# A two-layer transformer on one core: loops written out, first DMAs in a new order, and tile 1's first attention and layer 1's folding moved into tile 0's U and G steps

## The chip, the core and the metric

The kernel runs on one core of a Trainium2 chip. The metric is the device time of one execution in microseconds, which is the median of several runs. A profile is one further execution, with a trace of every engine: TensorE (PE, its weight loads PEld), VectorE (DVE), ScalarE (ACT), GpSimd (POOL) and SyncE (SP), which here issues all DMAs.

## The reference

The input is x, 16 tiles of 512 tokens x 256 values, float32. With `ln` the layer norm without weights:

```
x = x + A0(ln x)    A0: q,k,v = x Wq^T+bq, x Wk^T, x Wv^T+bv; 16 heads of 16; phi(t) = silu(t * 16^-0.25) + 1
                        kv = sum over tokens of phi(k) v; out = phi(q) kv; out Wo^T + bo
x = x + F0(ln x)    F0: h = silu((x w1^T) s1) * ((x w2^T) s2)        256 -> 1024, w ternary
                        h = gelu((h h1^T) s3); h = gelu((h h2^T) s4)  1024 -> 1024 -> 1024
                        (h w3^T) s5                                   1024 -> 256
x = x + A1(ln x)    A1: one head over the tile's 512 tokens: softmax(q k^T / 16) v, then w_out
x = x + F1(ln x)    F1: tanh(x W a1 a2 + bias)
```

## The kernel before

The 16 tiles are independent. A tile's work is cut into steps, and each engine walks the same list of steps, in order, doing its own share of each. The letters before a colon say for which tile a step is: `a` and `n` the next tile's first attention and the start of its F0, none the present tile's F0, `c` the tile before, whose layer 1 is computed. Since each engine runs its queue in order, a step's place in the list sets what stands in front of what.

F0 takes a tile in two halves of 256 tokens. U steps (4 for a half) multiply by w1 and w2, G steps by h1, H steps by h2, W by w3. A float32 factor is split into a high and a low float32r part (ACT, DVE and POOL do so), and PE multiplies both: 16 matmuls of 256 columns in a U step, 16 x 2 in a G, H or W step. BST, BNO and BT are statistics, normalising and transposing of a half; AST, ANO, T, AKV0 to 3, AS, AQ, AM, AO the first attention; CST to CF layer 1. PSUM has two rings of four banks, `ffn_fill` (F0) and `att_fill` (all else); a semaphore of each bank tells when it is full and when it was taken (lines 346 to 367).

PROLOGUE computes tile 0's first attention, splits the weights of it (PREP) and folds layer 1's weight matrices into each other (FOLD0, WIDE, TAKE0, FOLD1, TAKE1: products of W, a1, a2, of w_q with w_k, of w_v with w_out). FIRST is tile 0's F0 with tile 1's first attention. Then a loop of 14 passes (`nc.Fori`, line 333) walks BODY, whose semaphore values and tile slots are computed in registers from the pass's number; then LAST and TAIL come, straight, with constants. PE has the whole of that twice, in an `If` (line 1036) and its `Else`: once with float32 matmuls and once with float32r matmuls.

Which one is taken is decided by the data. The five big weights go from their input to a scratch tensor in HBM (`bounce`) and from there to SBUF (`land`). LOOK steps then read the low halves of 2048 elements of each partition: DVE takes the maximum of 1280 (line 708), ACT the sum of squares of 768 (line 789). CHECK0 to CHECK3 (w1 and w2, h1, h2, w3) add these up over the partitions with one matmul by ones, DVE writes a flag (line 712), and PE loads it into a register (`value_load`, line 829) before the first step that uses the layer, and branches on it in each step of FIRST (line 830). These weights are ternary, so the float32r form runs.

SP issues all DMAs in order. They share one queue. It waits for a `bounce` before the `land` of the same weights. x is in four slots of SBUF, and the raw weights of layer 1 are in the slots of tiles 1 to 3 until FOLD is through; hence x of tiles 1 to 3 is loaded after that. The core's lines: 510 to 523 layer norm, 563 and 728 the split after T, 575, 580 and 737 U on DVE and ACT, 584, 586 and 746 G and H, 493 POOL's low part in U, 602, 603 and 751 AKV, 635 AO, 671 CF, 688 to 703 TAKE; on PE 808 all products of `product`, 847 G and H, 863 and 871 transposes, 905 W.

The list of a pass, PLAN, which is BODY; FIRST is its steps without those of `c`, each with its looks behind it:

```python
    U0 c:CST U1 U2 U3 c:CNO G0 c:T c:CB c:CQ G1 c:CV c:CZ G2 c:CS0 G3 c:CP0 c:CS1 c:CS2 c:CO0 c:CP1 c:CS3
    H0 c:CO1 c:CP2 H1 c:CO2 BST1 c:CP3 BNO1 a:AST H2 c:CO3 c:DST H3 BT1 c:DNO W0 c:T a:ANO U0 U1 c:CF a:T
    U2 U3 a:AB a:AKV0 a:AKV1 a:AKV2 G0 a:AKV3 G1 G2 a:AS a:AQ a:AM G3 a:AO H0 H1 n:BST0 n:BNO0 H2 H3 n:BT0
    W1
```

Of the kernel before, what the change touches and what calls it, by code (L numbers as in the profile page):

```python
# [34 lines left out]
P = 128  # L35
D = 256
# [102 lines left out]
def with_checks(steps, behind):

    out, behind = [], dict(behind)
    for s in steps:
        out.append(s)
        out += steps_from(behind.pop(s[:2], ""))
    return out
# [48 lines left out]
def before(value):  # L194
# [4 lines left out]
PROLOGUE = steps_from("""  # L199
    a:AST a:ANO a:AB PREP a:T a:AKV0 SCALE a:AKV1 a:AKV2 a:AKV3 a:AS a:AQ a:AM a:AO FOLD0 WIDE  # L200
    n:BST0 n:BNO0 TAKE0 n:BT0 FOLD1 LOOK00 TAKE1 LOOK01 CHECK0 LOOK10 LOOK11""")
FIRST = with_checks(only("", "a", "n"), {
    ("U", 1): "LOOK12", ("U", 2): "LOOK13", ("U", 3): "CHECK1", ("G", 0): "LOOK20", ("G", 1): "LOOK21 LOOK22",
    ("G", 2): "LOOK23", ("G", 3): "CHECK2 LOOK30", ("H", 0): "CHECK3"})
BODY = PLAN
# [4 lines left out]
def build(nc, a):  # L210
    with ExitStack() as ctx:
# [3 lines left out]
        def sem(name):  # L215
            return ctx.enter_context(nc.semaphore(name))
# [51 lines left out]

        values = [sb("values_hi", [P, NB, D], F32R), m_parts[:].rearrange("p h k d -> p (h k) d")]
        prob = kv_b[:].rearrange("p (r a) d -> p r (a d)", r=2)  # L270
        prob_t = hi_lo("prob_t", [P, NB, P])
        kv = sb("kv", [P, KD, P])
# [14 lines left out]
        raw_wq = gated[:, 0]  # L287
        raw = [x[:, 1 + n // 2, 2 * (n % 2):2 * (n % 2) + 2, :] for n in range(6)]
        raw_q, raw_k, raw_v, raw_out, raw_f, raw_a1 = raw
        spare = whole[:].rearrange("p a b n -> p (a b n)")  # L290
        raw_a2 = spare[:, 0:512].rearrange("p (k n) -> p k n", k=KD)
        t1 = gated[:, 1]
        bk_wide = spare[:, 512:768].rearrange("p (k n) -> p k n", k=KD)
        bv_wide = spare[:, 768:1024].rearrange("p (k n) -> p k n", k=KD)
        squares = kv_b[:].rearrange("p a d -> p (a d)")

# [3 lines left out]
        s = {n: sem(n) for n in names}  # L300
        x_loaded, x_stored = sem("x_loaded"), sem("x_stored")
        a_loaded, c_loaded, small_loaded = sem("a_loaded"), sem("c_loaded"), sem("small_loaded")
        w_bounced = [sem(f"{n}_bounced") for n in CHECKED]
        w_loaded = [sem(f"{n}_loaded") for n in CHECKED]
        consts, wide, all_checked = sem("consts"), sem("wide"), sem("all_checked")
# [25 lines left out]

        def walk_rest(eng, part):
            with nc.Fori(0, T - 2, engines=[eng.engine], hint_back_edge=True) as it:
                steps_of(part, BODY, Counts(phases[2], rate, it),
                         {"c": eng.snap(it % SLOTS), "": eng.snap((it + 1) % SLOTS),
                          "a": eng.snap((it + 2) % SLOTS), "n": eng.snap((it + 2) % SLOTS)})
            steps_of(part, LAST, Counts(phases[3]), {"c": (T - 2) % SLOTS, "": (T - 1) % SLOTS})
            steps_of(part, TAIL, Counts(phases[4]), {"c": (T - 1) % SLOTS})

        def walk(eng, part):  # L340
            walk_first(part)
            walk_rest(eng, part)

# [50 lines left out]
        @block.sync  # L394
        def _(sp):
            sp.dma_start(x[:, 0], x_in[0]).then_inc(x_loaded, 16)
            sp.dma_start(raw_wkv[:, :, 0:D], km("wk0T")).then_inc(a_loaded, 16)
            sp.dma_start(raw_wkv[:, :, D:2 * D], km("wv0T")).then_inc(a_loaded, 16)
            sp.dma_start(raw_wq, km("wq0T")).then_inc(a_loaded, 16)
            sp.dma_start(wo[:], km("wo0T")).then_inc(a_loaded, 16)  # L400
            sp.dma_start(rows[:, 0:5, :], a["rows"][None].broadcast_to([P, 5, D])).then_inc(small_loaded, 16)
            sp.dma_start(cols[:], a["cols"]).then_inc(small_loaded, 16)
            sp.dma_start(scales[:], a["scales"]).then_inc(small_loaded, 16)


            parts = [[("w1T", w12[:, 0]), ("w2T", w12[:, 1])], [("h1T", h1[:])], [("h2T", h2[:])], [("w3T", w3[:])]]

            def bounce(layer):
                for name, _ in parts[layer]:
                    sp.dma_start(a["scratch_" + name], a[name]).then_inc(w_bounced[layer], 16)  # L410

            def land(layer):
                sp.wait_ge(w_bounced[layer], 16 * len(parts[layer]))
                for name, tile in parts[layer]:
                    sp.dma_start(tile.bitcast(F32), a["scratch_" + name].rearrange("(k p) n -> p k n", p=P))\
                      .then_inc(w_loaded[layer], 16)

            for tile, name in ((raw_q, "L1_attn_w_q"), (raw_k, "L1_attn_w_k"), (raw_v, "L1_attn_w_v"),
                               (raw_out, "woutT"), (raw_f, "wfT"), (raw_a1, "L1_ffn_aux_weight1"),
                               (raw_a2, "L1_ffn_aux_weight2")):  # L420
                sp.dma_start(tile, km(name)).then_inc(c_loaded, 16)
            bounce(0)
            bounce(1)
            land(0)
            land(1)
            bounce(2)
            land(2)
            bounce(3)
            land(3)

            c = Counts(phases[0])
            for step in PROLOGUE:
                if step[:2] == ("FOLD", 1):
                    wait_taken(sp, c, "att_fill", 2)
                c.ahead(step)
            for t in range(1, SLOTS):
                sp.dma_start(x[:, t], x_in[t]).then_inc(x_loaded, 16)
                sp.wait_ge(x_loaded, 16 * (t + 1))

            with nc.Fori(0, T - SLOTS, engines=[sp.engine], hint_back_edge=True) as t:  # L440
                slot = sp.snap(t % SLOTS)
# [12 lines left out]
        def _(pool):  # L454
# [623 lines left out]
```

## Time and profile before

| | us |
|---|---|
| runs | 2123.40, 2119.36, 2122.65 (median 2122.65) |
| the profiled execution's own time | 2121.59 |
| its span in the profile | 2119.2 |

| engine | PE | PEld | DVE | ACT | POOL |
|---|---|---|---|---|---|
| busy, us | 2012.3 | 1935.5 | 1208.2 | 837.6 | 372.9 |

The span runs from the first to the last instruction of the profile; the own time has 2.4 us more. The mean granted clock of PE is 0.986 of the full one. Times in the views are microseconds from the start of the span. A row of windows gives the length, then busy time and instructions of PE, PEld, DVE, ACT, POOL, the granted clock, the DMA share and GB/s. "idle before <-releaser" is the time for which an engine had nothing running and what ended it; "issue" stands for time in which it waited for nothing that the profile shows. "PEldq" is PE's sequencer, which hands the instructions to the array.

### The profile page before, as it was taken

The page shows a single profiled execution, that of the slowest core. Times are in us where ns is not written, and L with a number is a line of the kernel's source. Part 1 is how long each engine was busy: PE and PEld are TensorE (multiplying, and loading weights), DVE is VectorE, ACT ScalarE, POOL GpSimd, SP SyncE. Part 2 cuts the span into 40 slices and gives each one's busy share as a digit, 9 for nine tenths or more (in the row PEclk, how much of TensorE's full clock was granted, in tenths as well). Part 3 has the DMA queues.
Part 4 walks back from the last instruction along what each step waited for, and adds up shares of the span by engine and source line. Part 5 has one row for each costly group of instructions (what it writes and reads, how often), then busy time and mean ns, then how long its engine had stood idle before and what let it go on. Part 6 is the DMA issues. An engine that isn't in the chain of part 4 may idle for free.

```text
span 2119.2 us, 40188 instructions
## 1 busy us (share of the span) xinstructions
PE 2012.3 (95%) x15484; PEld 1935.5 (91%) x15484; DVE 1208.2 (57%) x2881; ACT 837.6 (40%) x1538; POOL 372.9 (18%) x347
## 2 busy tenths in 40 slices
PE   6899999999999999999999999999999999999985
PEld 5898999999999998999999999998999999999985
DVE  5555656465565645656366564655656466565544
ACT  2334434344443434434344343444434344343422
POOL 1111211012121021211012121121211112121011
PEclk9999999999999999999999999999999999999997
DMA  9400000000000000000000000000000000000000
GB/s 365 180 3 2 21 1 11 11 1 21 1 21 2 1 21 2 21 1 11 11 1 21 2 21 1 1 21 1 21 1 1 21 1 11 2 11 1 2 11 10
DMA packets 24402, 45.99 MB, mean 22 GB/s; under 512 B 1152, under 2 KB 21376, under 8 KB 24064
## 3 DMA queue, kind: packets, MB, share of 16 engines
q1 hardware_dynamic: 24240, 43.41, 5.8%
q8 instruction: 153, 2.51, 0.5%
q14 instruction: 9, 0.07, 0.0%
HBM read 35.02 MB, written 19.92 MB: 26 GB/s over the span
## 4 chain that ended last, share of the span: by engine, by line
PE 80%; DVE 7%; POOL 4%; issue 4%; DMA 3%; ACT 2%; SPq 0%; DVEq 0%; POOLq 0%; ACTq 0%
PE ffn_fill L847 43%; PE att_fill L808 23%; PE ffn_fill L905 6%; PE ffn_fill L808 5%; POOL act_lo L493 3%; DVE whole L575 2%; PE att_fill L863 2%; PE att_fill L981 1%; DMA scratch_h2T<-in_h2T 1%; DMA scratch_h1T<-in_h1T 1%; POOL rstd_C L480 1%; DVE st L510 1%; DVE act_hi L580 1%; DMA h<-scratch_h2T 1%; PE ffn_fill L871 1%
## 5 line engine op out<-in xcount | busy, mean ns | idle before, releaser
L847 PE MATMUL ffn_fill<-act_hi,h 128*128 128x256 f32 x4096 | 989.5, 284 | 9.6 <-POOL act_lo L493 4.1
L847 PE MATMUL ffn_fill<-act_lo,h 128*128 128x256 f32 x4096 | 980.4, 281 | 0.0
L847 PEld LDWEIGHTS ffn_fill<-act_hi,h 128*128 128x128 f32 x4096 | 773.3, 189 | 17.0 <-POOL act_lo L493 7.3
L847 PEld LDWEIGHTS ffn_fill<-act_lo,h 128*128 128x128 f32 x4096 | 774.7, 189 | 3.7
L584 DVE CAST act_hi<-whole 128x512 fp32r<-128x512 f32 x256 | 109.9, 429 | 570.8 <-ACT whole L746 570.8
L746 ACT ACTIVATE whole<-ffn_fill,scales 128x256 f32<-128x256 f32 x512 | 215.2, 472 | 553.7 <-PE ffn_fill L847 552.8
L808 PE MATMUL ffn_fill<-half_hi,w 128*128 128x256 f32 x1024 | 260.7, 294 | 39.7 <-issue 29.9
L808 PE MATMUL ffn_fill<-half_lo,w 128*128 128x256 f32 x1024 | 255.3, 288 | 0.0
L808 PEld LDWEIGHTS ffn_fill<-half_hi,w 128*128 128x128 f32 x1024 | 201.2, 196 | 45.0 <-issue 35.2
L493 POOL TENSOR_TENSOR act_lo<-whole,act_hi 128x512 fp32r<-128x512 f32 x128 | 166.9, 1304 | 405.3 <-DVE act_hi L580 404.7
L480 POOL TENSOR_TENSOR rstd_B<-var_eps_B,minus_half 128x2 f32<-128x2 f32 x32 | 22.7, 709 | 1131.5 <-DVE var_eps_B L517 1131.5
L808 PEld LDWEIGHTS ffn_fill<-half_lo,w 128*128 128x128 f32 x1024 | 201.3, 197 | 0.0
L586 DVE TENSOR_TENSOR act_lo<-whole,act_hi 128x512 fp32r<-128x512 f32 x256 | 190.9, 746 | 8.8
L746 ACT ACT_TABLE_LOAD x92 | 118.0, 1283 | 163.2 <-PE ffn_fill L847 143.4
L737 ACT ACTIVATE gated<-ffn_fill,scales 128x256 f32<-128x256 f32 x256 | 105.9, 473 | 159.7 <-PE ffn_fill L808 159.0
L575 DVE SCALAR_TENSOR_TENSOR whole<-ffn_fill,scales,gated 128x256 f32<-128x256 f32 x256 | 111.8, 478 | 69.9 <-PE ffn_fill L808 64.6
L905 PE MATMUL ffn_fill<-w,act_hi 128*128 128x256 f32 x512 | 123.8, 285 | 0.0
L905 PE MATMUL ffn_fill<-w,act_lo 128*128 128x256 f32 x512 | 121.1, 279 | 0.0
L905 PEld LDWEIGHTS ffn_fill<-w,act_lo 128*128 128x128 f32 x512 | 96.6, 189 | 0.0
L905 PEld LDWEIGHTS ffn_fill<-w,act_hi 128*128 128x128 f32 x512 | 96.1, 188 | 0.0
L510 DVE BATCH_NORM_STATS2 st<-x 128x6 f32 (+1 forms) x256 | 91.2, 414 | 6.6 <-DMA x<-in_L_attn_x 5.0
L475 POOL TENSOR_TENSOR x<-x,rows 128x512 f32 (+1 forms) x64 | 85.2, 1352 | 21.0 <-DVE xn L523 18.0
(156 smaller groups left out, 3156.0 us busy)
## 6 DMA issues: line engine op xcount, KB each, us to landing
x<-in_L_attn_x SPq DMA_DIRECT2D x16, 512.0 KB, 3.8
out<-x SPq DMA_DIRECT2D x16, 512.0 KB, 3.7
h<-scratch_h1T SPq DMA_DIRECT2D x1, 4096.0 KB, 16.2
h<-scratch_h2T SPq DMA_DIRECT2D x1, 4096.0 KB, 13.8
w<-scratch_w1T SPq DMA_DIRECT2D x1, 1024.0 KB, 14.4
w<-scratch_w2T SPq DMA_DIRECT2D x1, 1024.0 KB, 16.5
w<-scratch_w3T SPq DMA_DIRECT2D x1, 1024.0 KB, 5.6
rows<-in_rows SPq DMA_DIRECT2D x1, 640.0 KB, 5.9
```

The source lines that it names most:

```text
L475: last = pool.tensor_tensor(xs[:, b:b + 2, :], xs[:, b:b + 2, :], row2(bias_row), ALU.add)
L480: pool.tensor_tensor(rstd_of[stage][:, :nb], var_eps_of[stage][:, :nb], minus_half[:, :nb], ALU.pow)\
L493: pool.tensor_tensor(act_lo[0][:, blocks], whole[:, n % WHOLES], act_hi[0][:, blocks].bitcast(F32), ALU.subtract).then_inc(s["ffn_ready"], 1)
L510: last = dve.bn_stats(st[:, b, :], xs[:, b, :])
L575: last = dve.scalar_tensor_tensor(whole[:, n % WHOLES, o, :], two(bank)[:, o, :], scales[:, 1, 2 * j + o:2 * j + o + 1], gated[:, j % 2, o ...
L584: dve.tensor_copy(act_hi[dst][:, blocks], whole[:, n % WHOLES]).then_inc(s["hi_ready"], 1)
L586: dve.tensor_tensor(act_lo[dst][:, blocks], whole[:, n % WHOLES], act_hi[dst][:, blocks].bitcast(F32), ALU.subtract).then_inc(s["ffn_ready ...
L737: last = act.activation(gated[:, j % 2, o, :], two(bank)[:, o, :], ACT.Silu, scale=scales[:, 0, 2 * j + o:2 * j + o + 1])
L746: last = act.activation(whole[:, n % WHOLES, o, :], two(bank)[:, o, :], ACT.Gelu, scale=scales[:, layer, 2 * j + o:2 * j + o + 1])
L808: last = pe.matmul(out, lhsT, rhs, start=n == 0, stop=n == len(pairs) - 1)
L847: last = pe.matmul(two(bank)[:, o, :], view(w), view(moving[:, k, :]), start=k == 0 and o == 0 and half == 0, stop=k == KH - 1 and half == ...
L905: last = pe.matmul(two(bank)[:, b, :], view(part_of[:, k, b * P:(b + 1) * P]), view(w3[:, k, :]), start=k == 0 and b == 0 and half == 0, s ...
```

## The change

- The loops of SP, POOL, DVE, ACT and of PE's `Else` are written out: 14 passes of BODY with constants for semaphore values and slots. PE's `If` side keeps its loop (`walk_rest_looped`).
- SP issues the copies of w1 and w2 ahead of layer 1's raw weights, x of tile 1 right behind them, then the rest; h1 and h2 land in two halves each with a semaphore of its own, w3 is copied before h2 and lands before it. x of tiles 2 and 3 still waits for FOLD1 to be taken. Layer 1's raw weights move: four to the slots of tiles 2 and 3, three to `staged`, memory that later holds `values_hi` and `prob_t`. Each slot of x has its own semaphore.
- PROLOGUE ends after tile 0's first attention, the two looks at w1 and w2 and CHECK0. Tile 1's first attention moves from the second half of FIRST to the first, between U0 and G2; FOLD0, WIDE, TAKE0, FOLD1, TAKE1 move from PROLOGUE into the G steps of FIRST. The looks at h1, h2 and w3 are placed anew. The second half of FIRST has no attention steps any more.
- ACT's squares go to a corner of `act1_hi` for w1, w2 and h1 (`early_squares`).

```diff
 PROLOGUE = steps_from("""
-    a:AST a:ANO a:AB PREP a:T a:AKV0 SCALE a:AKV1 a:AKV2 a:AKV3 a:AS a:AQ a:AM a:AO FOLD0 WIDE
-    n:BST0 n:BNO0 TAKE0 n:BT0 FOLD1 LOOK00 TAKE1 LOOK01 CHECK0 LOOK10 LOOK11""")
-FIRST = with_checks(only("", "a", "n"), {
-    ("U", 1): "LOOK12", ("U", 2): "LOOK13", ("U", 3): "CHECK1", ("G", 0): "LOOK20", ("G", 1): "LOOK21 LOOK22",
-    ("G", 2): "LOOK23", ("G", 3): "CHECK2 LOOK30", ("H", 0): "CHECK3"})
+    a:AST a:ANO a:AB PREP a:T a:AKV0 SCALE a:AKV1 a:AKV2 a:AKV3 a:AS a:AQ a:AM LOOK00 a:AO
+    n:BST0 LOOK01 n:BNO0 n:BT0 CHECK0""")
+FIRST = steps_from("""
+    U0 a:AST U1 a:ANO U2 a:T U3 LOOK10 a:AB a:AKV0 a:AKV1 LOOK11 a:AKV2 LOOK12 a:AKV3 LOOK13 CHECK1 a:AS a:AQ
+    G0 a:AM FOLD0 G1 TAKE0 a:AO WIDE G2 LOOK20 LOOK21 FOLD1 TAKE1 G3 LOOK22 LOOK23 CHECK2 LOOK30
+    H0 CHECK3 H1 BST1 BNO1 H2 H3 BT1 W0 U0 U1 U2 U3 G0 G1 G2 G3 H0 H1 n:BST0 n:BNO0 H2 H3 n:BT0 W1""")
...
-        act_hi = [sb(f"act{n}_hi", [P, KH, HT], F32R) for n in range(2)]
+        act0_hi = sb("act0_hi", [P, KH, HT], F32R)
+        squares_at = -(-nc.sbuf_base // 32) * 32
+        act_hi = [act0_hi, sb("act1_hi", [P, KH, HT], F32R)]
+        early_squares = nc.alloc_sbuf_tensor_at("early_squares", [P, SQUARED], F32, offset=squares_at)
...
-        values = [sb("values_hi", [P, NB, D], F32R), m_parts[:].rearrange("p h k d -> p (h k) d")]
+        staged_at = -(-nc.sbuf_base // 32) * 32
+        staged = sb("staged", [P, 4, KD, D])
+        values = [nc.alloc_sbuf_tensor_at("values_hi", [P, NB, D], F32R, offset=staged_at), m_parts[:].rearrange("p h k d -> p (h k) d")]
         prob = kv_b[:].rearrange("p (r a) d -> p r (a d)", r=2)
-        prob_t = hi_lo("prob_t", [P, NB, P])
+        prob_t = [nc.alloc_sbuf_tensor_at(f"prob_t_{part}", [P, NB, P], F32R, offset=staged_at + 4 * P * NB * n)
+                  for n, part in ((2, "hi"), (3, "lo"))]
...
-        raw = [x[:, 1 + n // 2, 2 * (n % 2):2 * (n % 2) + 2, :] for n in range(6)]
-        raw_q, raw_k, raw_v, raw_out, raw_f, raw_a1 = raw
-        spare = whole[:].rearrange("p a b n -> p (a b n)")
-        raw_a2 = spare[:, 0:512].rearrange("p (k n) -> p k n", k=KD)
-        t1 = gated[:, 1]
-        bk_wide = spare[:, 512:768].rearrange("p (k n) -> p k n", k=KD)
-        bv_wide = spare[:, 768:1024].rearrange("p (k n) -> p k n", k=KD)
-        squares = kv_b[:].rearrange("p a d -> p (a d)")
+        raw_q, raw_k, raw_v, raw_out = (x[:, 2 + n // 2, 2 * (n % 2):2 * (n % 2) + 2, :] for n in range(4))
+        raw_f, raw_a1, raw_a2, t1 = (staged[:, n] for n in range(4))
+        bk_wide, bv_wide = (raw_a1[:, n].rearrange("p (k n) -> p k n", k=KD) for n in range(KD))
+        late_squares = kv_b[:].rearrange("p a d -> p (a d)")
...
-        x_loaded, x_stored = sem("x_loaded"), sem("x_stored")
+        x_loaded, x_stored = [sem(f"x_loaded{n}") for n in range(SLOTS)], sem("x_stored")
...
-        w_loaded = [sem(f"{n}_loaded") for n in CHECKED]
+        w_loaded = [[sem(f"{n}_loaded{half}") for half in range(2)] for n in CHECKED]
...
-        def walk_rest(eng, part):
+        def walk_rest(part):
+            straight = Counts(phases[2])
+            for it in range(T - 2):
+                straight.seen = {}
+                steps_of(part, BODY, straight, {"c": it % SLOTS, "": (it + 1) % SLOTS,
+                                                "a": (it + 2) % SLOTS, "n": (it + 2) % SLOTS})
+            straight.seen = {}
+            steps_of(part, LAST, straight, {"c": (T - 2) % SLOTS, "": (T - 1) % SLOTS})
+            straight.seen = {}
+            steps_of(part, TAIL, straight, {"c": (T - 1) % SLOTS})
+        def walk_rest_looped(eng, part):
             with nc.Fori(0, T - 2, engines=[eng.engine], hint_back_edge=True) as it:
                 steps_of(part, BODY, Counts(phases[2], rate, it),
...
+        def landed(j):
+            return w_loaded[j // 10][j % 10 * 2 // LOOKS[j // 10]]
...
-            parts = [[("w1T", w12[:, 0]), ("w2T", w12[:, 1])], [("h1T", h1[:])], [("h2T", h2[:])], [("w3T", w3[:])]]
-            def bounce(layer):
-                for name, _ in parts[layer]:
+            def bounce(layer, *names):
+                for name in names:
                     sp.dma_start(a["scratch_" + name], a[name]).then_inc(w_bounced[layer], 16)
-            def land(layer):
-                sp.wait_ge(w_bounced[layer], 16 * len(parts[layer]))
-                for name, tile in parts[layer]:
-                    sp.dma_start(tile.bitcast(F32), a["scratch_" + name].rearrange("(k p) n -> p k n", p=P))\
-                      .then_inc(w_loaded[layer], 16)
-            for tile, name in ((raw_q, "L1_attn_w_q"), (raw_k, "L1_attn_w_k"), (raw_v, "L1_attn_w_v"),
-                               (raw_out, "woutT"), (raw_f, "wfT"), (raw_a1, "L1_ffn_aux_weight1"),
+            def land(layer, half, name, tile):
+                k = tile.shape[1]
+                sp.dma_start(tile.bitcast(F32), a["scratch_" + name].rearrange("(k p) n -> p k n", p=P)[:, :k]
+                             if half == 0 else
+                             a["scratch_" + name].rearrange("(k p) n -> p k n", p=P)[:, -k:])\
+                  .then_inc(w_loaded[layer][half], 16)
+            bounce(0, "w1T", "w2T")
+            sp.dma_start(x[:, 1], x_in[1]).then_inc(x_loaded[1], 16)
+            for tile, name in ((raw_f, "wfT"), (raw_a1, "L1_ffn_aux_weight1"), (raw_q, "L1_attn_w_q"),
+                               (raw_k, "L1_attn_w_k"), (raw_v, "L1_attn_w_v"), (raw_out, "woutT"),
                                (raw_a2, "L1_ffn_aux_weight2")):
                 sp.dma_start(tile, km(name)).then_inc(c_loaded, 16)
-            bounce(0)
-            bounce(1)
-            land(0)
-            land(1)
-            bounce(2)
-            land(2)
-            bounce(3)
-            land(3)
+            sp.wait_ge(w_bounced[0], 16 * 2)
+            land(0, 0, "w1T", w12[:, 0])
+            land(0, 1, "w2T", w12[:, 1])
+            bounce(1, "h1T")
+            bounce(3, "w3T")
+            sp.wait_ge(w_bounced[1], 16)
+            land(1, 0, "h1T", h1[:, :KH // 2])
+            land(1, 1, "h1T", h1[:, KH // 2:])
+            bounce(2, "h2T")
+            sp.wait_ge(w_bounced[3], 16)
+            land(3, 0, "w3T", w3[:])
+            sp.wait_ge(w_bounced[2], 16)
+            land(2, 0, "h2T", h2[:, :KH // 2])
+            land(2, 1, "h2T", h2[:, KH // 2:])
             c = Counts(phases[0])
-            for step in PROLOGUE:
+            for step in PROLOGUE + FIRST:
                 if step[:2] == ("FOLD", 1):
-                    wait_taken(sp, c, "att_fill", 2)
+                    wait_taken(sp, c, "att_fill", 0)
+                    wait_taken(sp, c, "att_fill", 1)
                 c.ahead(step)
-            for t in range(1, SLOTS):
-                sp.dma_start(x[:, t], x_in[t]).then_inc(x_loaded, 16)
-                sp.wait_ge(x_loaded, 16 * (t + 1))
-            with nc.Fori(0, T - SLOTS, engines=[sp.engine], hint_back_edge=True) as t:
-                slot = sp.snap(t % SLOTS)
+            for t in range(2, SLOTS):
+                sp.dma_start(x[:, t], x_in[t]).then_inc(x_loaded[t], 16)
+            for t in range(T - SLOTS):
                 sp.wait_ge(s["out_ready"], t + 1)
-                sp.dma_start(x_out[t], x[:, slot]).then_inc(x_stored, 16)
-                wait_apart(sp, x_stored, 16 * t + 16)
-                wait_apart(sp, x_loaded, 16 * t + 16 * SLOTS)
-                sp.dma_start(x[:, slot], x_in[t + SLOTS]).then_inc(x_loaded, 16)
+                sp.dma_start(x_out[t], x[:, t % SLOTS]).then_inc(x_stored, 16)
+                sp.wait_ge(x_stored, 16 * t + 16)
+                sp.dma_start(x[:, t % SLOTS], x_in[t + SLOTS]).then_inc(x_loaded[t % SLOTS], 16)
...
-                    wait_apart(dve, x_loaded, c.value("a_tile", 1) * 16)
+                    n = c.value("a_tile")
+                    dve.wait_ge(x_loaded[n % SLOTS], 16 * (n // SLOTS + 1))
...
-                    act.activation(squares[:, :SQUARED], low_halves(j)[0], ACT.Square,
+                    act.activation(early_squares[:] if j < 20 else late_squares[:, :SQUARED], low_halves(j)[0], ACT.Square,
...
             with pe.If(inexact != 0):
                 plain["form"] = lambda ap: ap.bitcast(F32)
-                walk_rest(pe, part)
+                walk_rest_looped(pe, part)
             with pe.Else():
                 plain["form"] = lambda ap: ap
-                walk_rest(pe, part)
```

## Rows read from the trace of the kernel before

**Rows 1.** The page's parts 1, 3, 6: busy; instruction queue; h2's landing
```profile
PE 2012.3 (95%) x15484; PEld 1935.5 (91%) x15484; DVE 1208.2 (57%) x2881; ACT 837.6 (40%) x1538; POOL 372.9 (18%) x347
...
q8 instruction: 153, 2.51, 0.5%
...
h<-scratch_h2T SPq DMA_DIRECT2D x1, 4096.0 KB, 13.8
```

**Rows 2.** Timeline of PE, some first matmuls: start, length, what, [idle before <-releaser]
```profile
85.22 0.39 PE L847 MATMUL ffn_fill<-act_hi,h 128*128 128x256 f32 x1 [1.52 <-DVE flag L712]
...
165.95 0.36 PE L808 MATMUL ffn_fill<-half_hi,w 128*128 128x256 f32 x1 [2.60 <-issue]
...
292.79 0.36 PE L808 MATMUL ffn_fill<-half_hi,w 128*128 128x256 f32 x1 [1.96 <-issue]
...
299.45 0.38 PE L808 MATMUL ffn_fill<-half_hi,w 128*128 128x256 f32 x1 [0.74 <-DVE whole L575]
...
1822.31 0.36 PE L808 MATMUL ffn_fill<-half_hi,w 128*128 128x256 f32 x1 [2.20 <-issue]
...
1947.02 0.28 PE L808 MATMUL ffn_fill<-half_hi,w 128*128 128x256 f32 x1
...
1953.40 0.36 PE L808 MATMUL ffn_fill<-half_hi,w 128*128 128x256 f32 x1 [0.55 <-DVE whole L575]
```

**Rows 3.** What PE waited for in 14 passes: us, times, longest
```profile
PE ffn_fill L808 <- issue: 29.9, 14, 2.6
PE att_fill L863 <- DVE kv_b L671: 9.4, 14, 0.7
```

**Rows 4.** Lines 333 (loop), 1036 (If): ns min/median/max, starts
```profile
L333 PEldq COMPARE_BRANCH  x14: 87/3496/3867, 288.9 to 1945.3; - x14
...
L1036 PEldq COMPARE_BRANCH  x1: 3721/3721/3721, 161.8 to 161.8; - x1
```

**Rows 5.** Windows: us, busy per engine, granted clock, DMA share, GB/s
```profile
1694.30:1697.60 3.30, 3.30 (x18) 3.30 (x17) 0.02 (x1) 0.84 (x2) 0.00 (x0) 0.50 0.00 0
...
1946.00:1950.00 4.00, 4.00 (x37) 4.00 (x36) 2.20 (x4) 0.84 (x2) 0.00 (x0) 1.00 0.02 4
...
292.79:417.68 124.89, 123.23 (x964) 118.81 (x964) 72.75 (x176) 52.10 (x95) 23.26 (x21) 1.00 0.03 10
```

**Rows 6.** What PE waited for up to 163.4 us
```profile
PE att_fill L808 <- DVE lowsum L708: 5.7, 3, 2.9
PE ffn_fill L847 <- DVE flag L712: 3.3, 2, 1.8
```

**Rows 7.** DVE's groups by line up to 163.4: xcount, busy, mean ns, idle
```profile
L708 DVE TENSOR_REDUCE lowsum<-h 128x1 f32<-128x1280 uint16 x8 | 11.7, 1479 | 7.3 <-DMA h<-scratch_h1T 3.7 <-DMA h<-scratch_h2T 3.6
L584 DVE CAST act_hi<-whole 128x512 fp32r<-128x512 f32 x16 | 6.8, 426 | 38.8 <-ACT whole L746 38.8
L575 DVE SCALAR_TENSOR_TENSOR whole<-ffn_fill,scales,gated 128x256 f32<-128x256 f32 x16 | 6.9, 474 | 0.5 <-PE ffn_fill L808 0.5
L580 DVE CAST act_hi<-whole 128x512 fp32r<-128x512 f32 x8 | 4.2, 528 | 0.3
L602 DVE TENSOR_TENSOR kv_b<-att_fill,rows 128x256 f32<-128x256 f32 x8 | 3.4, 424 | 8.8 <-ACT xn L751 8.8
```

**Rows 8.** DVE's timeline at two places
```profile
32.76 0.69 DVE L635 TENSOR_TENSOR x<-att_fill,x 128x512 f32<-128x512 f32 x1 [0.68 <-PE att_fill L808]
...
50.55 1.49 DVE L708 TENSOR_REDUCE lowsum<-h 128x1 f32<-128x1280 uint16 x1 [3.72 <-DMA h<-scratch_h1T]
```

**Rows 9.** Windows of the start; the last two: att_fill on PE
```profile
47.82:53.91 6.09, 6.09 (x32) 5.88 (x32) 3.36 (x4) 3.27 (x9) 0.00 (x0) 0.62 1.06 397
...
102.55:163.35 60.80, 60.80 (x479) 58.86 (x477) 30.13 (x64) 25.17 (x44) 8.67 (x8) 1.00 0.01 3
...
32.72:37.80 5.08, 5.08 (x25) 1.00 0.98 360
...
90.95:163.35 72.40, 15.59 (x88) 1.00 0.03 10
```

More of the change, by code:

```diff
@@ L136, in only @@
     return [s for s in PLAN if s[2] in whose]
[L139 to L145, printed above, removed]
 CHECKED = ["w12", "h1", "h2", "w3"]
@@ L338, in walk_rest, with walk @@
             steps_of(part, TAIL, Counts(phases[4]), {"c": (T - 1) % SLOTS})
-        def walk(eng, part):
+        def walk(part):
             walk_first(part)
-            walk_rest(eng, part)
+            walk_rest(part)
         def wait(eng, which, value):
@@ L395, in _ @@
         def _(sp):
-            sp.dma_start(x[:, 0], x_in[0]).then_inc(x_loaded, 16)
+            sp.dma_start(x[:, 0], x_in[0]).then_inc(x_loaded[0], 16)
             sp.dma_start(raw_wkv[:, :, 0:D], km("wk0T")).then_inc(a_loaded, 16)
@@ L500, in part @@
                     last.then_inc(s["out_ready"], 1)
-            walk(pool, part)
+            walk(part)
         @block.vector
@@ L705, in part @@
                 elif kind == "LOOK":
-                    dve.wait_ge(w_loaded[j // 10], 16 * (2 if j < 10 else 1))
+                    dve.wait_ge(landed(j), 16)
                     dve.tensor_reduce(lowsum[:, j // 10, 2 * (j % 10):2 * (j % 10) + 1], low_halves(j)[1],
@@ L716, in part @@
                         dve.tensor_reduce(flag[:, 4:5], flag[:, 0:4], AX.X, ALU.add).then_inc(all_checked, 1)
-            walk(dve, part)
+            walk(part)
         @block.scalar
@@ L785, in part @@
                 elif kind == "LOOK":
-                    act.wait_ge(w_loaded[j // 10], 16 * (2 if j < 10 else 1))
+                    act.wait_ge(landed(j), 16)
                     wait(act, s["look_sum"], c.value("look_sum"))
-                    act.activation(squares[:, :SQUARED], low_halves(j)[0], ACT.Square,
+                    act.activation(early_squares[:] if j < 20 else late_squares[:, :SQUARED], low_halves(j)[0], ACT.Square,
                                    accum_out=lowsum[:, j // 10, 2 * (j % 10) + 1:2 * (j % 10) + 2])\
@@ L795, in part @@
                     act.activation(wq[0][:], raw_wq, ACT.Copy).then_inc(s["split_hi"], 1)
-            walk(act, part)
+            walk(part)
         @block.tensor
@@ L1037, in _ @@
                 plain["form"] = lambda ap: ap.bitcast(F32)
-                walk_rest(pe, part)
+                walk_rest_looped(pe, part)
             with pe.Else():
                 plain["form"] = lambda ap: ap
-                walk_rest(pe, part)
+                walk_rest(part)
 def kernel(**inputs):
```

## The prediction

> **What bounds the kernel now.** Read the shares first: TensorE (PE) is busy for 95% of the span and VectorE (DVE) for 57% [rows 1]. So PE bounds the steady part, and a change pays there only if it shortens PE's work, its idle time, or its time at half clock. The change leaves a tile's matmuls alone, so idle time and clock are what is left.
>
> The kernel has two parts. PE starts the first loop pass at 165.95 us and the last at 1822.31 us; the remaining pass, LAST and TAIL follow [rows 2]. Within the passes the idle list is short. PE waits for "issue" 29.9 us in 14 places and for DVE's L671 9.4 us; the rest is small [rows 3]. The issue waits stand at the seam ahead of each pass, at its first matmul: 2.60, 1.96, ..., 2.20 us [rows 2]. What PE's sequencer does there is in the rows of line 333. The branch back took 3496 ns in the median on PE; its minimum, 87 ns, is the one that is not taken, at 1945.3 us. At that point the code runs on straight into LAST, and PE goes from L905 to L808 at 1947.02 without any idle time [rows 2, 4]. So the gap belongs to the taken branch, not to work that is late.
>
> The second cost is the clock. In six of the passes 3.3 us shortly behind the seam run at 0.50 of full clock, 1.2 instead of 2.4 GHz (the last of the six is shown, with 18 matmuls); the 4.0 us around the seam without a gap hold 37, and the clock stays at 1.00 [rows 5]. A pass without a dip takes 124.89 us from its first matmul to the next seam; twelve passes with their gaps take 1529.5, from 292.79 to 1822.31 [rows 2, 5].
>
> The start is another regime: weights are still landing, and PE idles where DVE's looks at them (L708, 1.48 us each) and the flags stand in front of it: 5.7 and 3.3 us [rows 6, 7].
>
> **The change part by part: the loops.** There are 14 issue waits. The first (2.60) follows the `If` of line 1036, whose branch took 3721 ns. That `If` remains, so this wait stays. Thirteen go: 29.9 - 2.6 = 27.3 us. The dips: 1529.5 less twelve of those gaps (27.3 - 1.96 = 25.3) less 12 x 124.89 leaves 5.5 us, and with the gaps gone I let the dips go too. Next is what is late once a seam has no gap. LAST shows it: U2 waits 0.55 us for `whole`, where a pass waits 0.74 [rows 2]. Its register operations are gone as well, as they will be in all passes. I count 0.2 us for U2 and under 0.1 for G0 in each of 14 passes, 3 us in all; the bounds are 0 and 6. DVE's L671 wait does not move: DVE's queue there is filled by the work of U1, not by registers. On POOL, ACT and SP the branches take 0.05 us and lie beside PE's work, so they are worth nothing. Sum for the loops: 27.3 + 5.5 + 3 = 35.8 us gained.
>
> The instruction queue moved 153 packets, 2.51 MB [rows 1], which is 64 bytes for each of 39,200 instructions, and 40,188 were executed. So the loop's code is already fetched anew in each pass, and straight code asks for no more.
>
> The Trainium skill, "Advanced Engine Details and Errata", section "Control Flow Timing", puts a compare-and-branch at about 108 ns. By that, thirteen branches would be worth 1.4 us and the whole result would be about 2127. The untaken one (87 ns) agrees with it; the taken ones (3496) do not, and I go by them.
>
> **The first DMAs.** They change order, not volume. Ahead of h1's landing (50.5 us before, where DVE's wait for it ends [rows 8]) now stand two more transfers, x1 (0.5 MB) and w3's copy (1 MB). 4 MB of h2 took 13.8 us to land [rows 1], so about 3.4 us a MB: h1 is in at about 55.5. w3's landing comes ahead of h2's too, 8.5 us in all, so h2 is in by about 84 instead of 75.1. w1 and w2 are copied ahead of the seven small weights, and land by 30 instead of 39.5. No wait of SP holds x2 and x3 back from their first use, which is past the start.
>
> **Tile 0, up to U0.** Until PE's end of AO (32.7) nothing moves; LOOK00 goes where DVE idled for AO's first product. DVE is through AO at 33.45 [rows 8]. Then follow statistics (1.2) and LOOK01 (1.4) to 36.05, normalising (0.7) to 36.8, PE's transposes, ACT's and DVE's halves (0.5 + 0.6 + 0.7) to 38.7, the flag (0.16), and 1.0 until PE's first matmul. U0 starts at **39.8**, 8 us sooner than before [rows 9]. But FOLD0 (5.1 us of PE [rows 9]) and FOLD1 (an estimate from it, 5.0) are still undone, and PE idles about 6 us between AO and U0, where they stood before. That should bring half clock, as shorter idling did before, when the 32 matmuls of U0 and U1 took 6.09 us at a clock of 0.62 [rows 9]; at full clock they take 3.9.
>
> **U0 to G0.** Now DVE is the bound, since it runs in order and gets everything at once. From U0's products at half clock (39.8 + 3.2 = 43.0) it owes: U four times (0.86 + 0.53) 5.6; AST 2.0; ANO 1.4; T 1.3; AKV four times 0.75 (L602, and a second of that size) = 3.0; LOOK10 to LOOK13 4 x 1.48 = 5.9 less overlaps, 5.6 [rows 7]. That is 18.8, with 1 for waits (POOL's power, PE's transposes), so LOOK13 ends at 62.8. PE's CHECK1 waits for it, and behind it in PE's order stand AS (1.7) and AQ (2.9). G0 starts at **67.7**. PE's work since 39.8 was 19 us, 21 at the mixed clock: 7 us idle. h1's landing (55.5) is 3 us ahead of LOOK12, about 58.5, and does not decide.
>
> **G0 to H0.** PE: four G at 3.9, AM 0.7, FOLD0 5.1, AO 2.9, FOLD1 5.0 = 29.3. AO's second half needs the bank that TAKE0 empties behind DVE's G1, 1.3 idle. PE ends G3 at 98.3. Here the order of the steps costs: LOOK22 and LOOK23 stand on DVE behind G3's own work, and CHECK2 on PE stands ahead of H0. ACT 0.9, DVE 1.1, two looks 2.9, product and flag 0.4, and 0.8 to the first matmul: H0 at **104.4**, 6 us idle.
>
> **H0 to the loop.** Before, from 85.22 to 163.35 (165.95 less its 2.60), 78.1 us [rows 2]. Off it come tile 1's attention (att_fill 15.6 [rows 9], less CHECK3's 0.3 and about 1.0 that PE overlaps at its seams: 14.3) and 1.7 of half clock (H0's stretch). On it go 1.0 (U2 and G0 wait, with no T between the U steps) and 1.7 of half clock after the 6 us: 64.8. Loop at 169.2 instead of 163.35, so the start **loses 5.8 us**. Its bounds: none of the 7 + 6 idle nor H0's dip, 14.7 better, so a gain of 9; 6 worse if DVE's casts and adds slow beside POOL (L580 took 0.43 or 0.83) or h2 and h1 land late, a loss of 12.
>
> **Sum.** 2119.2 - 35.8 + 5.8 = 2089.2 us of span. The profiled execution took 2121.6, 2.4 more than its span, and the median of the three runs is 1.05 above that: 2092.6, say **2092.5**.
>
> **Rivals.** (1) The start gains: the overlaps I deny do come, because DVE's looks find holes. For it: DVE is idle 38.8 us for ACT's `whole` over the start [rows 7]. Against: those holes lie in G and H steps, not between U0 and CHECK1. The bound above gives 2078. (2) The start is worse than walked, 6 us more and two dips of 1.7 beside: 2102. For it: PE idles in three places of 6 us and each can bring a dip. (3) Slower than before: the 2.1 us at the seam is the supply of code, not the branch, and straight code pays it as often, at the 16 KB packets; then the loops give nothing, the start costs 5.8, and the time is 2128.5. It decides from one such wait a tile upwards. For it: those packets are fetched either way. Against: the untaken seam, and the straight code from 102.55 to 163.35, in which PE idles for nothing [rows 9]. (4) The unrolled branch of line 1036 isn't taken (`inexact` true), the looped copy runs, and only the start changes: 2128. Against: the flag comes from the same weights.
>
> The Trainium skill, "Runtime: NRT & Kernel Launch", section "Instruction fetch mechanics", says that fetching is sequential in blocks of 16 KiB, that crossing one is mostly hidden, and that a taken branch out of the window stalls. Rival 3 has no place in it; the rows of lines 333 and 1036 agree.
>
> **How the numbers follow.** Forecast 0.62 (its own range 2084 to 2100), rival 1 0.20, rival 2 0.12, rivals 3 and 4 together 0.04, anything else 0.02. 0.2% is 4.2 us, about what can be told here from no change. Faster 0.95, same 0.01, slower 0.04. The range for 8 in 10 runs from 2077 (rival 1) to 2105 (rival 2 with the register gain at 0).
>
> **What would show it.** Right: no issue wait at W1's end but the first; passes of 124.7 us; clock 1.00 from the first pass to TAIL. U0 near 39.8, G0 near 67.7 behind CHECK1, about 6 us of PE idle ahead of H0, W1's end near 169. Wrong: issue waits inside straight code; an end of W1 below 160 (rival 1) or above 175 (rival 2); DVE's LOOK10 or LOOK12 waiting for DMA.

## The result, and the profile after

The changed kernel takes 2128.2 us (median of 7 runs, 2127.9 to 2130.2) against 2122.6 before, ratio 1.0031 with a 95% interval of 1.0022 to 1.0040. Faster was forecast, 2092.5; it is slower. The profiled span is 2128.4 against 2119.2.

The page, busy times and instruction queue, as in [rows 1]: the same work, and 17 instruction packets fewer.

```profile
PE 2012.7 (95%) x15484; PEld 1930.3 (91%) x15484; DVE 1191.6 (56%) x2881; ACT 831.8 (39%) x1534; POOL 373.9 (18%) x347
...
q8 instruction: 136, 2.23, 0.4%
```

Cut the 9.2 us by where things end on PE. W1 of FIRST ends at 174.99 us (177.38 less 2.40, below) against 163.35: the start loses 11.6. From there to LAST's first matmul it is 1782.6 against 1783.7. LAST and TAIL are 1.3 shorter. So **the passes, which should have given 35.8, gave 1.1**. PE's timeline at the places to which [rows 2] answer:

```profile
36.32 0.77 PE L885 MATMUL ffn_fill<-ident,xn_b 128*128 128x128 f32 x4 [3.76 <-DVE xn_b L536]
...
39.69 0.58 PE L822 MATMUL ffn_fill<-half_hi,w 128*128 128x256 f32 x1 [2.48 <-issue]
...
49.75 1.31 PE L877 MATMUL att_fill<-ident,xn 128*128 128x128 f32 x8 [2.07 <-DVE xn L536]
...
65.50 0.59 PE L822 MATMUL att_fill<-lowsum,ones 128*128 128x8 f32 x2 [5.22 <-DVE lowsum L722]
...
108.83 0.39 PE L822 MATMUL att_fill<-lowsum,ones 128*128 128x8 f32 x2 [4.97 <-DVE lowsum L722]
110.32 0.58 PE L861 MATMUL ffn_fill<-act_hi,h 128*128 128x256 f32 x1 [1.09 <-DVE flag L726]
...
177.38 0.55 PE L822 MATMUL ffn_fill<-half_hi,w 128*128 128x256 f32 x1 [2.40 <-issue]
```

The seam gaps are gone, as forecast, all but the first (2.40, issue). What PE waits for in the 14 passes instead, to which [rows 3] answer:

```profile
PE att_fill L995 <- ACT kv_b L790: 21.4, 28, 1.3
PE att_fill L822 <- DVE prob_t_lo L660: 10.3, 14, 0.7
PE ffn_fill L822 <- DVE whole L589: 7.7, 14, 0.6
PE att_fill L877 <- DVE kv_b L685: 5.4, 14, 0.4
```

The first two lines are new in the passes: 21.4 + 10.3 = 31.7 us, ahead of the transposes of CP0 (0.2 each) and CP1 (1.3), and ahead of CO0 (0.7). The third and fourth fell, as LAST showed for `whole`; the wait for L671 before, L685 now, fell from 9.4 to 5.4, which I had not counted. Two stretches of the start, and 127.01 us across the seam at 306.02, as long as a pass (granted clock is the third figure from the end), to which [rows 5] answer:

```profile
37.50:44.20 6.70, 4.51 (x21) 4.51 (x22) 1.37 (x4) 1.06 (x3) 0.00 (x0) 0.50 0.69 229
64.80:71.50 6.70, 6.00 (x23) 5.62 (x24) 1.23 (x3) 0.00 (x0) 0.00 (x0) 0.50 0.74 233
304.39:431.40 127.01, 123.61 (x967) 118.88 (x966) 72.75 (x179) 52.04 (x96) 23.29 (x21) 1.00 0.03 10
```

No pass after the first has half clock any more; the start has more of it, about 23 us in four stretches against 13 in three. A pass takes 127.05 us from first matmul to first matmul (mean of 12), against 127.46 before.

**Where the new waits come from.** ScalarE's (ACT) timeline in one pass of the kernel before: the exp of CS0 and of CS1, each behind a table load.

```profile
321.41 1.28 ACT L776 ACT_TABLE_LOAD   x1 [0.54 <-PE att_fill L808]
323.13 0.69 ACT L776 ACTIVATE kv_b<-att_fill,sm 128x512 f32<-128x512 f32 x1 [0.44 <-DVE sm L657]
...
327.02 1.28 ACT L776 ACT_TABLE_LOAD   x1 [0.47 <-PE att_fill L808]
328.92 0.69 ACT L776 ACTIVATE kv_b<-att_fill,sm 128x512 f32<-128x512 f32 x1 [0.61 <-DVE sm L657]
```

The table loads (1.28 us) while DVE still reduces the scores, and then the exp waits 0.44 and 0.61 for DVE's `exp_bias`. The first of the two places after:

```profile
336.32 1.28 ACT L790 ACT_TABLE_LOAD   x1 [2.31 <-DVE sm L671]
337.62 0.69 ACT L790 ACTIVATE kv_b<-att_fill,sm 128x512 f32<-128x512 f32 x1
```

Now the table load itself waits for DVE, and the exp comes behind it; CS1's waits 2.41 us in the same way. Count the operations of ACT's sequencer (ACTq) at the line that waits for `exp_bias`, before (line 774) and after (788):

```profile
L774 ACTq ALU_OP  x42: 35/35/35, 200.1 to 1861.4; - x42
L774 ACTq FUSED_REGOPS  x14: 37/37/37, 194.5 to 1850.9; - x14
L774 ACTq EVENT_SEMAPHORE  x8: 17/17/17, 1977.3 to 2092.5; - x8
```

```profile
L788 ACTq EVENT_SEMAPHORE  x64: 17/17/17, 209.2 to 2102.0; - x64
```

In the loop the line gave 42 + 14 = 56 register operations, one for each of the 4 CS steps of 14 passes, and no wait of its own; in LAST and TAIL, and in straight code everywhere, it gives a wait of its own, EVENT_SEMAPHORE, of which there are 64.

### The profile page after: what moved, and what is told of

The parts are those of the page before. It is cut to its first block, busy times and chain, and to the rows that moved or that the text cites. A ratio compares the mean times of both kernels' runs of the same rounds, so it can differ in the third digit from the quotient of the medians.

```text
span 2128.4 us, 37458 instructions
## 1 busy us (share of the span) xinstructions
PE 2012.7 (95%) x15484; PEld 1930.3 (91%) x15484; DVE 1191.6 (56%) x2881; ACT 831.8 (39%) x1534; POOL 373.9 (18%) x347
## 4 chain that ended last, share of the span: by engine, by line
PE 81%; DVE 9%; ACT 6%; issue 2%; POOL 1%; DMA 0%; DVEq 0%; ACTq 0%; POOLq 0%
PE ffn_fill L861 41%; PE att_fill L822 22%; PE ffn_fill L822 9%; PE ffn_fill L919 6%; PE att_fill L877 2%; DVE whole L589 2%; ACT L790 2%; ACT whole L760 1%; DVE st L523 1%; PE att_fill L995 1%; ACT kv_b L790 1%; POOL act_lo L506 1%; DVE sm L665 1%; ACT L760 1%; DVE act_hi L594 1%
## 5 line engine op out<-in xcount | busy, mean ns | idle before, releaser
L822 PE MATMUL ffn_fill<-half_hi,w 128*128 128x256 f32 x1024 | 253.6, 288 | 13.2 <-DVE whole L589 8.3
L822 PE MATMUL ffn_fill<-half_lo,w 128*128 128x256 f32 x1024 | 249.2, 284 | 0.0
L822 PEld LDWEIGHTS ffn_fill<-half_hi,w 128*128 128x128 f32 x1024 | 196.3, 192 | 16.1 <-issue 16.1
L760 ACT ACT_TABLE_LOAD x90 | 115.5, 1283 | 213.0 <-PE ffn_fill L861 212.7
L822 PEld LDWEIGHTS ffn_fill<-half_lo,w 128*128 128x128 f32 x1024 | 197.0, 192 | 0.0
L600 DVE TENSOR_TENSOR act_lo<-whole,act_hi 128x512 fp32r<-128x512 f32 x256 | 177.3, 693 | 8.8
L523 DVE BATCH_NORM_STATS2 st<-x 128x6 f32<-128x256 f32 x256 | 91.0, 413 | 5.2 <-DMA x<-in_L_attn_x 4.6
L822 PE MATMUL att_fill<-values_hi,prob_t_hi 128*128 128x256 f32 x256 | 73.7, 288 | 14.1 <-DVE prob_t_lo L660 14.0
```

Of the source, the lines that this page charges most:

```text
L523: last = dve.bn_stats(st[:, b, :], xs[:, b, :])
L600: dve.tensor_tensor(act_lo[dst][:, blocks], whole[:, n % WHOLES], act_hi[dst][:, blocks].bitcast(F32), ALU.subtract).then_inc(s["ffn_ready ...
L760: last = act.activation(whole[:, n % WHOLES, o, :], two(bank)[:, o, :], ACT.Gelu, scale=scales[:, layer, 2 * j + o:2 * j + o + 1])
L822: last = pe.matmul(out, lhsT, rhs, start=n == 0, stop=n == len(pairs) - 1)
```

## Experiments

The theory (A): a semaphore wait goes to the next instruction in the code. In the loop the wait for the full bank fell to the register operation that computes `exp_bias`'s value, and `exp_bias`'s own wait to the exp, with the table load ahead of it. With constants nothing stands between the two waits; the first goes to the exp, the second becomes an operation ahead of the table load. The rival (B): without the seam gap the chain from CS to CP is simply 2 us too late.

**e1_order**, the changed kernel with the two waits swapped:

```diff
-                    bank, out = filled(act, c, "att_fill", 0)
                     act.wait_ge(s["exp_bias"], c.value("exp_bias", 1))
+                    bank, out = filled(act, c, "att_fill", 0)
```

> The changed kernel with the two waits of ACT's exp step (CS) swapped: first exp_bias, then the full bank. Theory A: in straight code the wait for exp_bias became an operation of its own ahead of the exp's table load (1.28 us), and the full bank's wait rides on the instruction; swapped, the table loads under cover of the wait. PE's idle ahead of CO0 (0.73), CP1 (1.32) and CP0 (0.21) goes in 14 passes and in LAST, 15 x 2.2 = 33 us, and TAIL gives 1.3 more: about 2094. Rival B: with the seam gap gone, the chain CS to CP on DVE and ACT is simply late by 2 us, and the table is not in it; then 2128, and the two PE gaps stay.

Measured: 2106.3 (0.9921, 0.9904 to 0.9937), passes of 125.59. A's direction, two thirds of its size (21.9 us of 34). The waits for ACT's exp are gone from the passes; that ahead of CO0 grew from 0.73 to 1.07 us:

```profile
PE att_fill L822 <- DVE prob_t_lo L660: 15.1, 14, 1.1
```

ACT's timeline shows what is next: the gelu of G3 has the same order, and its table load waited for PE.

```profile
457.51 1.28 ACT L790 ACT_TABLE_LOAD   x1 [0.52 <-PE att_fill L822]
459.25 0.69 ACT L790 ACTIVATE kv_b<-att_fill,sm 128x512 f32<-128x512 f32 x1 [0.46 <-DVE sm L671]
...
461.30 1.28 ACT L760 ACT_TABLE_LOAD   x1 [1.27 <-PE ffn_fill L861]
462.60 0.84 ACT L760 ACTIVATE whole<-ffn_fill,scales 128x256 f32<-128x256 f32 x2
```

**e2_loops** and **e3_loops_order**: the kernel before with only its loops written out (walk_rest as in the diff of the change, SP's loop too), and the same with the swap.

> The kernel before with its loops written out on all engines and nothing else (old start, old DMA order, old order of waits). If the two parts of the change add up: the changed kernel's 2128.2 less the 11.6 us that its start loses (W1's end at 174.99 against 163.35) = 2117, or 2 to 6 us under the kernel before; a pass takes 127.05 us from first matmul to first matmul, with PE idle 0.73 ahead of CO0 and 1.32 ahead of CP1. If the new start is to blame for the gaps in the passes (another place of buffers or semaphores), they are missing here and the time is about 2087.

> As e2_loops, with the two waits of ACT's exp step swapped. Theory A: both the seam gaps and the exposed table loads are gone, passes of 124.9 us, clock 1.00 through the passes: 2117 - 33 = about 2084 to 2088. Rival B: as e2_loops, 2117.

Measured: 2117.7 (0.9977, 0.9967 to 0.9987) and 2095.0 (0.9870, 0.9853 to 0.9886). The two parts of the change add up: the loops alone give 5.7 (against 2123.45 before, measured beside them), the new start loses 11.6, and the difference, 5.9, is near the 5.6 that the change lost. W1's end is at 163.15, and e2's passes have the same waits as the changed kernel's:

```profile
PE att_fill L991 <- ACT kv_b L786: 21.5, 28, 1.3
PE att_fill L818 <- DVE prob_t_lo L656: 10.2, 14, 0.7
```

The swap gave 22.7 here, as on the changed kernel, and not the 29 to 33 that were expected.

**e4_before_order**, the swap in the looped kernel:

> The kernel before, loops kept, with the same two waits swapped. In the loop, waits on a register's value come in the order of the code and the last one rides on the instruction, so the swap should do harm there. Theory A: exp_bias now stands ahead of the table load in the 14 passes, PE idles about 2 us a pass at CO0 and CP1 on top of the seam gap: 14 x 2.2 = 31 slower, less 3 in LAST and TAIL: about 2150. Rival B (the table is not in the chain): 2122.

Measured: 2120.8 (0.9986, 0.9975 to 0.9996). The expected harm did not come. ACT in a pass:

```profile
450.83 1.28 ACT L776 ACT_TABLE_LOAD   x1 [0.52 <-PE att_fill L808]
452.58 0.69 ACT L776 ACTIVATE kv_b<-att_fill,sm 128x512 f32<-128x512 f32 x1 [0.46 <-DVE sm L657]
```

The exp still carries `exp_bias`'s wait. Swapped, no register operation follows that wait, so here too two waits fall to the exp, and the one coded first rides. I had taken it to be the last one. The other one, for the full bank, shows in ACT's sequencer at the line of `filled`, first before, then in this run: 64 more, one for each CS step of 16 tiles.

```profile
L367 ACTq EVENT_SEMAPHORE  x238: 17/17/17, 25.7 to 2055.5; - x119
...
L367 ACTq EVENT_SEMAPHORE  x302: 17/17/17, 27.3 to 2093.1; - x151
```

LAST and TAIL, straight in both, took 167.7 us instead of 172.2, as A has it for straight code; the passes took 127.76 on average, 0.3 more. The null in the passes therefore fits A as stated above, and does not by itself tell it from B; e11 below does.

**e5_order2** and **e6_loops_order2**: the same swap in G and H too, on the changed kernel and on e3.

```diff
                 elif kind in ("G", "H"):
-                    act.wait_ge(s["ffn_ready"], c.value("ffn_ready", 1 - WHOLES))
                     bank, out = filled(act, c, "ffn_fill", 0)
+                    act.wait_ge(s["ffn_ready"], c.value("ffn_ready", 1 - WHOLES))
```

> e1_order, and in the G and H steps ACT's two waits swapped too (first the full bank, then ffn_ready). In e1_order the gelu's table load still stands behind the wait for PE's full bank (EVENT_SEMAPHORE, ACT_TABLE_LOAD, ACTIVATE), which delays prob_t_hi and leaves PE 1.08 us idle ahead of CO0. Theory A (the wait that is coded first rides on the instruction, the second stands ahead of its table load): that gap goes in 14 passes and LAST, 15 x 1.08 = 16: about 2090, passes near 124.5 us. Rival: CO0 waits for DVE's part of the chain, then 2106 and 125.6.

> The same two swaps on the kernel before with its loops written out and its old start (e3_loops_order, 2095.0). Theory A: 16 less, 2079, with passes near 124.5. Rival: 2095.

Measured: 2083.8 (0.9817, 0.9801 to 0.9833) and **2072.0** (0.9757, 0.9741 to 0.9773), passes of 124.06 in both, where 124.7 was forecast for the change. This swap gave 22.5 and 23.0, where 16 was expected. All that PE still waits for in e5's passes, seam to seam, beside the first seam:

```profile
PE ffn_fill L822 <- DVE whole L589: 7.7, 14, 0.6
PE att_fill L877 <- DVE kv_b L685: 5.3, 14, 0.4
PE ffn_fill L861 <- POOL act_lo L506: 2.5, 14, 0.2
```

**e11_loop_exposed**, the reverse: loops kept, order of waits kept, only the register operation moved out from between them.

```diff
+                    bias_at = c.value("exp_bias", 1)
+                    if not isinstance(bias_at, int):
+                        bias_at = act.to_reg(bias_at)
                     bank, out = filled(act, c, "att_fill", 0)
-                    act.wait_ge(s["exp_bias"], c.value("exp_bias", 1))
+                    act.wait_ge(s["exp_bias"], bias_at)
```

> The kernel before, loops kept, order of waits kept; only the register with exp_bias's value is computed ahead of the wait for the full bank instead of between the two waits. Theory A (a wait rides on the next instruction in the code, here a register operation, and two waits with nothing between them both fall to the exp, where the first rides and the second stands ahead of the table load): the table load now stands behind exp_bias in the loop too, PE idles about 0.7 and 1.3 us at CO0 and CP1 and 0.2 at CP0 in 14 passes, 31 us: about 2150. If the seam gap, straight code or e4_before_order's null mean that the table load is not in the chain of a looped pass: 2122.

Measured: 2158.8 (1.0176, 1.0152 to 1.0200), passes of 129.95. ACT in a pass, its sequencer at the line that waits for `exp_bias` (8 such operations before), and PE's waits:

```profile
324.35 1.28 ACT L779 ACT_TABLE_LOAD   x1 [2.31 <-DVE sm L657]
325.64 0.69 ACT L779 ACTIVATE kv_b<-att_fill,sm 128x512 f32<-128x512 f32 x1
...
L777 ACTq EVENT_SEMAPHORE  x64: 17/17/17, 194.6 to 2126.7; - x64
```

```profile
PE ffn_fill L811 <- issue: 31.1, 14, 2.5
PE att_fill L984 <- ACT kv_b L779: 21.4, 28, 1.3
PE att_fill L811 <- DVE prob_t_lo L646: 10.3, 14, 0.8
```

The looped kernel with its seam gaps now has the changed kernel's waits beside them, to 0.1 us. B is out: neither straight code nor the missing gap is needed for them.

**The start.** e7 to e10 build on e5_order2 (W1's end 172.8). e7_looks: `TAKE1 LOOK22 LOOK23 G3 CHECK2` for `TAKE1 G3 LOOK22 LOOK23 CHECK2`.

> e5_order2 with LOOK22 and LOOK23 placed ahead of G3 instead of behind it. If PE's idle ahead of H0 (4.97 us in the changed kernel) is DVE's two looks standing behind G3's own work: 3 us of it go, and 1 to 2 us of half clock behind it: W1's end 4 to 5 us earlier than in e5_order2, about 2086. If PE waits there for h2's landing, nothing moves.

Measured: 2079.0 (0.9789, 0.9773 to 0.9805), W1's end 170.5. PE's wait for the looks ahead of H0 fell from 4.97 in the changed kernel to 1.17, while the flag's wait rose from 1.09 to 1.58. So the 3 us of idle time went, but W1's end came 2.3 us earlier instead of 4 to 5; the medians differ by 4.8, the profiled executions by 1.9:

```profile
104.80 0.39 PE L822 MATMUL att_fill<-lowsum,ones 128*128 128x8 f32 x2 [1.17 <-DVE lowsum L722]
...
106.78 0.39 PE L861 MATMUL ffn_fill<-act_hi,h 128*128 128x256 f32 x1 [1.58 <-DVE flag L726]
```

e8_check1: `a:AKV3 a:AS LOOK13 a:AQ CHECK1` for `a:AKV3 LOOK13 CHECK1 a:AS a:AQ`.

> e5_order2 with CHECK1 behind AS and AQ instead of ahead of them, and LOOK13 between them. In the changed kernel PE idles 5.22 us ahead of CHECK1 and then runs AS and AQ at half clock (7.3 us instead of 4.6). If LOOK13 on DVE is what it waits for: AS and AQ run in that idle time, G0 starts 3 to 5 us earlier, about 2086. If PE waits for h1's landing or the AKV products, nothing moves.

Measured: 2084.6 (0.9819, 0.9803 to 0.9835), no gain. The idle time moved, to AS and to G0:

```profile
62.84 3.78 PE L822 MATMUL att_fill<-xn,kv_b 128*128 128x128 f32 x16 [3.64 <-DVE xn L617]
...
73.32 0.39 PE L861 MATMUL ffn_fill<-act_hi,h 128*128 128x256 f32 x1 [2.66 <-DVE flag L726]
```

AS waits for AKV3's part on DVE, and G0 for a flag that DVE writes behind AQ's part. It is DVE's sum that bounds this stretch, not where PE meets it: in the changed kernel DVE idles for only 1.76 us between 43.59 and 65.44.

e9_fold0: `a:AO FOLD0 n:BST0 ... CHECK0 TAKE0` in PROLOGUE, both out of the G steps. e10_fold_looks: that and e7's.

> e5_order2 with FOLD0 back between AO and BST0, as in the kernel before, and TAKE0 behind CHECK0. PE idles 3.77 + 2.44 us between AO and U0 in e5_order2, and DVE idles about 5 us behind the flag. If that idle time is only missing work: FOLD0's 5.1 us of PE go into it, U0 starts about 1.5 us later, AO's wait for TAKE0 (1.3) goes, and less runs at half clock: W1's end 4 to 6 us earlier, about 2079. If the chain AO, BST0, LOOK01, BNO0, BT0 is all that counts and FOLD0 only delays it, nothing is gained.

> e7_looks (2079.0) with the same move of FOLD0 and TAKE0. If the two repairs of the start add up: 2074 to 2075, still 2 to 3 above e6_loops_order2 (2072.0), whose start is the old one. If moving FOLD0 gains nothing: 2079.

Measured: 2077.5 (0.9789, 0.9773 to 0.9806) with W1's end at 167.2, and 2071.6 (0.9759, 0.9742 to 0.9775) with 165.8. PE's idle time ahead of U0 held FOLD0 and U0 came no later (39.5). With both repairs the new start is on a par with the old one (e6, 2072.0) and no better: W1's end is 1.8 us later than e6's, LAST and TAIL are 1.6 shorter.

## Why the prediction was wrong

- *"Next is what is late once a seam has no gap. LAST shows it"*: this step failed, and with it the term of 35.8 us for the loops, of which 1.1 came. I read of LAST only what stands around its seam. The waits of 0.21, 0.74 and 1.32 us stood in LAST before, 32 to 40 us behind its first matmul, and in no pass:

```profile
1979.50 0.66 PE L981 MATMUL att_fill<-ident,kv_b 128*128 128x128 f32 x4 [0.21 <-ACT kv_b L776]
...
1983.64 0.36 PE L808 MATMUL att_fill<-values_hi,prob_t_hi 128*128 128x256 f32 x1 [0.74 <-DVE prob_t_lo L646]
...
1986.63 0.66 PE L981 MATMUL att_fill<-ident,kv_b 128*128 128x128 f32 x4 [1.32 <-ACT kv_b L776]
```

  They were put down to nothing, and 14 of each came with the straight code. Experiments e1, e5 and e11 show their cause: a wait that stood behind ACT's table load now holds it up. Against the forecast a pass is 127.05 - 124.7 = 2.35 us too long, 33 us in 14. With both swaps it gets 127.05 - 124.06 = 3.0 shorter, or 42 in 14, more than the 31.7 of idle time shown; the rest stands in the traces as busy time of PE, 123.6 us a pass against 122.9 for the same matmuls.
- *"27.3"* of seam gaps and *"5.5"* of dips: right; no issue wait but the first, and no half clock in the passes behind the first. U2's wait fell by 0.2 as forecast; that for L671, which "does not move", by 0.3 a pass.
- *"3 us in all"* for the register operations: U2's 0.2 was right, but the term was incomplete in kind. The register operations also decided which instruction a wait fell to.
- The start: U0 at 39.8 (39.7 measured), G0 to H0 36.7 (37.1), H0 to W1's end 64.8 (64.7), landings of h1 and h2 early enough (no wait of DVE for them). U0 to G0 was mis-sized, 27.9 forecast against 33.6, and makes the start's loss 11.6 instead of 5.8. LOOK13 ended at 65.4, not 62.8, and AS and the first part of AQ ran at half clock behind PE's 5.22 us of idle, both in 7.3 instead of 4.6. DVE's TENSOR_SCALARs took two to four times as long beside POOL:

```profile
48.18 2.38 DVE L536 TENSOR_SCALAR xn<-x,mv_A,rstd_A 128x256 f32<-128x256 f32 x4
...
57.75 1.14 DVE L617 TENSOR_SCALAR xn<-xn 128x256 f32<-128x256 f32 x1
...
59.14 1.05 DVE L617 TENSOR_SCALAR xn<-xn 128x256 f32<-128x256 f32 x1
...
61.85 0.28 DVE L617 TENSOR_SCALAR xn<-xn 128x256 f32<-128x256 f32 x1
...
63.97 1.47 DVE L722 TENSOR_REDUCE lowsum<-h 128x1 f32<-128x1280 uint16 x1
```

  (L536: four in 2.38, of which the first, beside POOL, took 1.42 and the others 0.40. L617: 1.14 and 1.05 beside POOL's bias add from 57.45 to 60.05, 0.28 behind it; in the whole trace 20 of its 64 touch no instruction of POOL and took 0.28, the others took 0.56 to 1.14.) Together these three operations took 2.6 us longer than alone, as much as LOOK13 was late. No run takes POOL's work away, so this cause rests on the trace. "6 worse if DVE's casts and adds slow beside POOL (L580 took 0.43 or 0.83) or h2 and h1 land late" was in the bounds of the range; it came in size, through these operations, while the casts kept their 0.43.
- Rival 3 had the right time, 2128.5, by the wrong mechanism: its waits inside straight code are not issue waits, and 136 instruction packets did no harm. That the loops give next to nothing and the start loses did happen; the code's supply is not in it. Rival 4 gave 2128 too, and is out: the straight copy ran, as the 13 seams without a gap show. Rival 2's first term, a start 6 us worse, came true; the rest of it didn't. The 2127 that the prediction gives for cheap branches is near as well, by luck: it leaves out the 3 us for registers, and the seams did give 27.3. No rival held what took place.

The rule of the Trainium skill, "Runtime: NRT & Kernel Launch", section "Instruction fetch mechanics", is that fetching on in sequence is mostly hidden and that a taken branch out of the window stalls. The traces agree: 13 seams without a branch have no issue wait, and with one they had 27.3 us.

## What to carry to other kernels

When registers turn into constants, look again at every instruction with two waits and a table load: the wait that ends last should ride on the instruction, behind the table load, and the other stand ahead of the load. In these runs the wait that rides is the one coded first, so code the one that ends last first. A stretch of the same code that already runs in the new form (a peeled last pass) is the best forecast there is, but it has to be read to its end, wait by wait. And of steps moved to fill another engine's idle time, add up what the engine beside it (here DVE) must do in that stretch before counting on it.

## What the runs showed of the hardware

A taken back edge cost PE about 2.1 us of idle time (27.3 us in 13), and 3.3 us of half clock came behind 6 of the 13; neither came at the same seams in straight code. An ACT table load took 1283 ns in all 31 places of the exp. Of two waits pending ahead of an ACTIVATE with its table load, the one coded first rode on the ACTIVATE and the other became an operation of its own ahead of the load, in the loop (e4, e11) as in straight code.

In the changed kernel's start half clock came behind idle times of 3.76, 2.07, 5.22 and 4.97 us, and one short stretch of it behind the `If`'s 2.40. In the kernels with the old start (before, e2, e3, e4, e6, e11) the `If`'s 2.2 to 2.6 us brought none; why was not tested.
